# Masks, maxima and output products in fewer VectorE instructions, with finer waits in the norms' moments

## What is computed

```python
def _mha(x, kv, Wq, Wk, Wv, mask, causal):          # block 0, a = 0 and 1
    ...
    lengths = jnp.sum(energy[:, :, 0, :] != 0, axis=-1)
    energy = jnp.where(cols[None, None, None, :] >= lengths[:, :, None, None], -jnp.inf, energy)
...
    scores = jnp.where(key_mask[None, :, None, :] == 0.0, NEG, scores)   # block 3, a = 5 to 7
    attn = jax.nn.softmax(scores, axis=-1)
    query_mask = jnp.sign(jnp.abs(jnp.sum(q, axis=-1)))
    attn = attn * query_mask[None, :, :, None]
    out = jnp.einsum('hbqk,hbkd->hbqd', attn, Vh)
    out = out.transpose(1, 2, 0, 3).reshape(B, Sq, d)
    out = out + q
    return _layer_norm(out, gamma, beta)
```

## Time and profile before

| | |
|---|---|
| median of 3 runs | 1087.1 us (1087.01 to 1087.42) |
| profiled execution, span from first to last instruction | 1085.1 us |
| median above that span | 2.0 us |
| PE busy | 1005.6 us, 93% |
| PEld busy | 725.6 us, 67% |
| DVE busy | 840.9 us, 77%, 2336 instructions |
| ACT busy | 635.8 us, 59% |
| POOL busy | 320.4 us, 30% |

### The profile page before, as it was taken

The page is one execution under the profiler, slowest core; times in us unless marked ns, Lnnn a source line. Parts: engine busy times, 40 slices in busy tenths (PEclk is TensorE's granted clock), DMA queues, the critical chain, the costliest instruction groups (busy, mean ns, idle before and its releaser), DMA issues.

```text
span 1085.1 us, 38818 instructions
## 1 busy us (share of the span) xinstructions
PE 1005.6 (93%) x16923; PEld 725.6 (67%) x16957; DVE 840.9 (77%) x2336; ACT 635.8 (59%) x938; POOL 320.4 (30%) x405
## 2 busy tenths in 40 slices
PE   8889988899999999999999998889999999998996
PEld 5657665576777677767776776556767677677674
DVE  5897999867476756789878899999567774679986
ACT  5346565567777464555645655556777766464652
POOL 4022245511000113346450313553011020336531
PEclk9999999999999999999979999999999999999998
DMA  7000000000000000000010000000000000000001
GB/s 255 3 22 23 2 3 3 2 2 2 3 3 3 12 9 14 11 2 2 2 31 2 3 13 3 2 2 2 3 2 3 3 3 3 1 2 2 2 2 40
DMA packets 13722, 13.60 MB, mean 13 GB/s; under 512 B 617, under 2 KB 13170, under 8 KB 13298
## 3 DMA queue, kind: packets, MB, share of 16 engines
q1 hardware_dynamic: 13554, 11.11, 3.2%
HBM read 9.01 MB, written 2.10 MB: 10 GB/s over the span
## 4 chain that ended last, share of the span: by engine, by line
PE 42%; DVE 28%; ACT 5%; issue 3%; POOL 2%; POOLq 0%; DVEq 0%; ACTq 0%
PE pair L708 8%; DVE mx L1363 7%; PE pair L916 7%; PE pair L911 5%; PE pair L782 4%; PE pair L695 4%; PE pair L935 3%; DVE stats L1085 3%; PE pair L815 2%; DVE Y L1164 2%; ACT PT L1011 2%; PE pair L702 2%; PE pair L683 2%; DVE Y L1108 2%; PE pair L949 2%
## 5 line engine op out<-in xcount | busy, mean ns | idle before, releaser
L1011 ACT ACTIVATE PT<-pair 128x1024 f32<-128x1024 f32 x184 | 180.3, 1029 | 124.8 <-PE pair L916 115.7
L1363 DVE TENSOR_REDUCE mx<-pair 128x16 f32<-128x1024 f32 x184 | 218.4, 1215 | 42.1 <-PE pair L916 41.6
L916 PEld LDWEIGHTS pair<-KQ 32*128 32x128 f32 (+3 forms) x4416 | 170.7, 157 | 37.6 <-DVE mx L1363 3.4
L916 PE MATMUL pair<-KQ 32*128 32x128 f32 (+3 forms) x4416 | 180.0, 254 | 2.4 <-DVE mx L1363 1.0
L708 PE MATMUL pair<-xf,W_all 128*128 128x512 f32 x336 | 177.4, 623 | 3.2 <-ACT xf L977 1.0
L1390 POOL TENSOR_SCALAR ve<-mv 128x4 f32<-128x4 f32 x64 | 17.0, 265 | 503.3 <-DVE mv L1088 432.5
L683 PE MATMUL pair<-warm 128*128 128x512 bf16 (+3 forms) x581 | 113.4, 395 | 17.8 <-DVE Y L1164 7.8
L977 ACT ACTIVATE KQ<-pair,c 128x512 f32<-128x512 f32 x160 | 100.3, 692 | 42.9 <-PE pair L708 42.2
L935 PE MATMUL pair<-PT,V 128*32 128x64 f32 x5120 | 94.2, 221 | 2.2 <-ACT PT L1011 0.7
L977 ACT ACTIVATE V<-pair 64x512 f32<-64x512 f32 x128 | 79.1, 618 | 26.5 <-PE pair L815 24.7
L935 PEld LDWEIGHTS pair<-PT,V 128*32 128x32 f32 x5120 | 78.3, 110 | 22.2 <-issue 8.7
(11 more groups left out here) (122 smaller groups left out, 1824.0 us busy)
## 6 DMA issues: line engine op xcount, KB each, us to landing
W_all<-weights SPq DMA_DIRECT2D x1, 2880.0 KB, 13.7
Xin<-x SPq DMA_DIRECT2D x8, 256.0 KB, 3.6
C<-ctx SPq DMA_DIRECT2D x8, 256.0 KB, 4.1
out<-X SPq DMA_DIRECT2D x8, 256.0 KB, 2.5
row<-rows SPq DMA_DIRECT2D x1, 1024.0 KB, 6.1
c<-const SPq DMA_DIRECT2D x1, 504.0 KB, 5.5
W_all<-weights SPq DMA_DIRECT2D x1, 192.0 KB, 2.9
c<-const SPq DMA_DIRECT2D x1, 80.5 KB, 2.0
```

Source lines behind the costliest of these rows:

```text
L916: last[u] = pe.matmul(banked[u // 2][:, at:at + 2 * S], stationary[rows_, seq].rearrange("p r t -> p (r t)"), moving[rows_, seq].rearrange ...
L1011: act.activation(PT[:, place, :], banks.of("B", a, s, v)[:], ACT.Exp, scale=float((D // (2 * PAIRS[a])) ** -0.5)).then_inc(*banks.drain((" ...
L1363: dve.tensor_reduce(dst, banks.of("A", a, s, v)[:].rearrange("p (u m t) -> p u m t", u=2, t=S), AX.X, ALU.max).then_inc(*banks.drain(("A", ...
```

## The change

The order table is untouched. The edits:

- **moments**: each statistics counts as an event of its own, and each aggregation waits for its own statistics instead of the last. In step z each statistics waits for its own j of X.
- **nm**: one scalar_tensor_tensor over all 128 partitions, mx times -1 times the table half, which is 1 at the partition's own place and 0 at the other; so it also writes the zeros.
- **lm, km**: one tensor_tensor over all 128 partitions each. lm compares with the table place (position at the own place, -1 at the other, where no length is below it) and yields 1; the factor -BIG moves into the tables passed and beyond, which lrow and kms now multiply by. km multiplies by the table gone.
- **outputs** for the last three attentions: rq is left out. Instead of one product of 256 elements there are two of 128 (j apart), each PSUM times qm as a scalar per partition, times rd.
- POOL's 16 memsets of nm8, lm8, nm2, lm2 go, and DVE's wait for them.
- The float constants grow from 161 to 174 columns.

```diff
-CONST32 = [("ident", 128), ("side8", 2), ("side2", 2), ("par8", 2), ("par2", 2), ("pos", 1),
-           ("own", 8), ("half", 2), ("strip", 4), ("rows", 2), ("ownA", 8)]
+CONST32 = [("ident", 128), ("side8", 2), ("side2", 2), ("par8", 2), ("par2", 2), ("place", 2),
+           ("own", 8), ("half", 2), ("strip", 4), ("rows", 2), ("ownA", 8),
+           ("passed", 8), ("beyond", 2), ("gone", 2)]
...
+    c["place"] = np.where(c["half"], (p % S)[:, None], -1)
+    c["passed"], c["beyond"], c["gone"] = -BIG * c["ownA"], -BIG * c["rows"], -ABSENT * c["half"]
...
-                def moments(src, *tag):
+                def moments(src, *tag, made=None):
                     for j in range(NT):
-                        dve.bn_stats(stats[lane(tag)][:, j, :], src[:, j, :]).then_inc(*vec.mark("stats", *tag))
-                    dve.wait_ge(*vec.at("stats", *tag))
+                        if made:
+                            dve.wait_ge(*vec.at(*made, j))
+                        dve.bn_stats(stats[lane(tag)][:, j, :], src[:, j, :]).then_inc(*vec.mark("stats", *tag, j))
                     for j in range(NT):
+                        dve.wait_ge(*vec.at("stats", *tag, j))
                         dve.bn_aggr(mv[lane(tag)][:, j, :], stats[lane(tag)][:, j, :]).then_inc(*vec.mark("mv", *tag))
...
+                    if PAIRS[a] == 2:
+                        o = O[s].rearrange("p j (h d) -> p j h d", h=heads)
+                        for j in range(2):
+                            q = 2 * half + j
+                            dve.scalar_tensor_tensor(out=o[:, q], in0=t[:, j, :, 0:dh], scalar=qm[s][:, q:q + 1],
+                                                     in1=rd[s][:, q, 0:heads].unsqueeze(2).broadcast_to((P, heads, dh)),
+                                                     op0=ALU.mult, op1=ALU.mult
+                                                     ).then_inc(*banks.drain(use, vec, "O", a, s, half))
+                        return
...
-                    if name in ("nm", "lm", "km"):
-                        loaded(pool, "zero", s)
...
-                        dve.wait_ge(*vec.at("x2", a, s))
-                        moments(X[s], "n3", a, s)
+                        moments(X[s], "n3", a, s, made=("x2", a, s))
...
                     elif name == "lm":
-                        for h in range(2):
-                            dve.tensor_scalar(lm8[s][r[h], :, h, :],
-                                              banks.of(*use)[r[h], 0:8 * NB].rearrange("p (n h) -> p n h", h=2),
-                                              K32("pos")[r[h]], -BIG, ALU.is_le, ALU.mult
-                                              ).then_inc(*banks.drain(use, vec, "lm", a, s))
+                        shape = P, 4 * NB, 2, 2
+                        dve.tensor_tensor(lm8[s][:], banks.of(*use)[:, 0:8 * NB].rearrange("p (n h) -> p n h", h=2).unsqueeze(
+                            2).broadcast_to(shape), K32("place").unsqueeze(1).unsqueeze(3).broadcast_to(shape), ALU.is_le
+                            ).then_inc(*banks.drain(use, vec, "lm", a, s))
                     elif name == "km":
-                        for h in range(2):
-                            dve.tensor_scalar(lm2[s][r[h], :, h, :], k[r[h]], -ABSENT, None, ALU.mult
-                                              ).then_inc(*banks.drain(use, vec, "lm", a, s))
+                        shape = P, NB, 2, 2
+                        dve.tensor_tensor(lm2[s][:], banks.of(*use)[:, 0:NB].unsqueeze(2).unsqueeze(3).broadcast_to(shape),
+                                          K32("gone").unsqueeze(1).unsqueeze(3).broadcast_to(shape), ALU.mult
+                                          ).then_inc(*banks.drain(use, vec, "lm", a, s))
                     elif name == "nm":
-                        for h in range(2):
-                            dst = (nm8 if pairs == 8 else nm2)[s][r[h], :, :, h]
-                            src = mx[s][r[h], 0:NB * pairs].rearrange("p (n h) -> p n h", h=2)
-                            dve.tensor_scalar(dst, src, -1.0, None, ALU.mult).then_inc(*vec.mark("nm", a, s))
+                        n = NB * pairs
+                        dve.scalar_tensor_tensor(
+                            out=(nm8 if pairs == 8 else nm2)[s].rearrange("p n r h -> p (n r) h"),
+                            in0=mx[s][:, 0:n].unsqueeze(2).broadcast_to((P, n, 2)), scalar=-1.0,
+                            in1=K32("half").unsqueeze(1).broadcast_to((P, n, 2)), op0=ALU.mult, op1=ALU.mult
+                            ).then_inc(*vec.mark("nm", a, s))
...
-                    for buf in (nm8, lm8, nm2, lm2, V8_padded, V2):
+                    for buf in (V8_padded, V2):
```

More of the change, by code:

```diff
@@ L349, in constants @@
     eye = np.eye(P)
-    c = {"ident": eye, "ones3": (p < 3)[:, None] * np.ones(128), "pos": (p % S)[:, None]}
+    c = {"ident": eye, "ones3": (p < 3)[:, None] * np.ones(128)}
     for n, pairs in (("8", 8), ("2", 2)):
@@ L1161, in outputs @@
                         f = rq
-                    o = O[s][:, two].rearrange("p j (h r d) -> p (j h) r d", r=2, d=dh) if PAIRS[a] == 8 else O[s][
-                        :, two].rearrange("p j (h d) -> p j h d", h=heads)
+                    o = O[s][:, two].rearrange("p j (h r d) -> p (j h) r d", r=2, d=dh)
                     dve.tensor_tensor(o, t[:, :, :, 0:dh], by_head(f).unsqueeze(3).broadcast_to((P, *o.shape[1:])),
@@ L1272, in step @@
                                                      in1=X[s][:, j, :], op0=ALU.mult, op1=ALU.add
-                                                     ).then_inc(*vec.mark("x2", a, s))
-                        dve.wait_ge(*vec.at("x2", a, s))
-                        moments(X[s], "n3", a, s)
+                                                     ).then_inc(*vec.mark("x2", a, s, j))
+                        moments(X[s], "n3", a, s, made=("x2", a, s))
                     elif name == "n3":
@@ L1332, in step @@
                         dve.wait_ge(*banks.ready(*use))
-                        k = banks.of(*use)[:, 0:NB].unsqueeze(2).broadcast_to((P, NB, 2))
-                        for h in range(2):
-                            dve.tensor_scalar(lm2[s][r[h], :, h, :], k[r[h]], -ABSENT, None, ALU.mult
-                                              ).then_inc(*banks.drain(use, vec, "lm", a, s))
+                        shape = P, NB, 2, 2
+                        dve.tensor_tensor(lm2[s][:], banks.of(*use)[:, 0:NB].unsqueeze(2).unsqueeze(3).broadcast_to(shape),
+                                          K32("gone").unsqueeze(1).unsqueeze(3).broadcast_to(shape), ALU.mult
+                                          ).then_inc(*banks.drain(use, vec, "lm", a, s))
                     elif name == "nm":
@@ L1351, in step @@
                                           banks.of(*use)[0:n, 0:S].unsqueeze(1).broadcast_to((n, 8, S)),
-                                          K32("ownA" if name == "lrow" else "own")[0:n, :].unsqueeze(2).broadcast_to(
+                                          K32("own" if name == "mrow" else "ownA" if PAIRS[a] == 2 else "passed")[0:n, :].unsqueeze(2).broadcast_to(
                                               (n, 8, S)), ALU.mult).then_inc(*banks.drain(use, vec, done, a, s))
@@ L1355, in step @@
                             dve.tensor_tensor(kms[s][0:n], banks.of(*use)[0:n, 0:S].unsqueeze(1).broadcast_to((n, 2, S)),
-                                              K32("rows")[0:n, :].unsqueeze(2).broadcast_to((n, 2, S)), ALU.mult
+                                              K32("rows" if PAIRS[a] == 2 else "beyond")[0:n, :].unsqueeze(2).broadcast_to((n, 2, S)), ALU.mult
                                               ).then_inc(*banks.drain(use, vec, "kms", a, s))
```

1 line of the change is left out of this document (removed).

## The result

| | before | after |
|---|---|---|
| median of 4 runs, alternating on one chip | 1087.26 us (1087.01 to 1089.19) | 1057.14 us (1055.88 to 1057.40) |
| ratio | | 0.9727 [0.9706, 0.9748] |
| profiled execution, span | 1085.1 us | 1055.4 us |
| mean granted clock of TensorE in it | 0.986 | 0.994 |
| DVE busy | 840.9 us | 793.3 us |

What follows compares the result with a forecast made beforehand. PE, 93% busy, was taken as the bound, waiting partly on DVE. DVE savings of 56 us x 0.36 gave 20, perhaps 25 us on the path, discounted to 16: 1071 us from 1087.1, range 1062 to 1083.

Steps and rivals of the forecast that it cites:

- What bounds the kernel: Whole span: PE, 93% busy, bounds; DVE savings help mostly in stretches making up 485 of 1085 us.
- Nearly none: Expected sign in 240:640: almost no PE idleness left there, of 63 us over the whole span.
- The size on DVE: All edited DVE parts: 56 us of 841 saved from start to start, DVE busy near 795 us.
- The products' open operand: Last layers' output products, PSUM, SBUF and scalar: 6.1 us saved if no POOL stalls, 4.3 us lost otherwise; gain taken.
- The path: Share of DVE savings on the chain of waits: 0.36 of 56 us, reduced to 16 us off the span.
- The chain sum: DVE savings on the chain of waits: 56 x 0.36 = 20 us, perhaps 25, before any discount.
- The discount for what the next path takes: PE becomes next when DVE comes earlier: middle of two thirds of each bound, 13 and 17, taken as 16 us.
- rival 2: Whole span: the whole chain sum comes through, 25 us and a little more, 1060 us; chance 0.12.
- my own case: Whole span: 16 us faster, 1071 us, within 1063 to 1079; chance 0.62.
- PE did not close up at once: Denies the rival that only stretches with PE below 90% gain: 5 us, 1082 us; chance 0.16.
- Rival 3: Finer waits on DVE: even a met wait bars overlap, so they save nothing, 1074 us; chance 0.06.
- Rival 4: Last layers' output products: both per half stall on POOL over the port, making the kernel slower, 1100 us; chance 0.04.

Runs made afterwards that it cites:

- late pads: Kernel before with the finer waits alone, plus a spare 72-element DVE reduction after the last aggregation in each of 88 moments calls: 1077.52 us, 0.9966.
- n_negmax: Kernel before with only the negated maxima made by one instruction (memsets stay): 1078.33 us, 0.9918.
- am_again: Changed kernel with the moments' coarse waits (for the last statistics) put back, run beside the changed kernel: 1066.51 us, 0.9817.
- an_halves: Changed kernel with the negated maxima in two partition halves again, with their memsets: 1067.14 us, 0.9864.

## Why the prediction was wrong

**What bounds the kernel: right.** The gain lies where DVE is dense, and PE closed most of it up elsewhere. "Nearly none" of PE's idleness in 240:640 was too strong: 10 of the 57.7 us are there, and the largest part (24 us) is in 0:240, which I had not named.

**The size on DVE: right.** The sum of 56 us from start to start meant a busy time near 795; it is 793.3. By parts the single kernels show busy time down by 12.0 (finer waits; 11.5 forecast, of which 3 are gaps), 18.9 (nm; 24.6, of which some 4 are gaps), 11.6 (masks; 13.9, some 2.4 gaps) and 3.9 (products; 6.1, some 1.7 gaps). The 12.0 hold the 3 us that are not the edit's. nm takes 284 and 192 ns in the median for 0.28 and 0.18, the small lm 186 for 0.18, the products 347 for 0.344, lm 287 for 0.28.

**The products' open operand: the bound taken was right.** 96 instructions lie between 341 and 352 ns, though 37 of them run beside a POOL operation of over 0.6 us. So neither PSUM with one SBUF tensor nor the scalar per partition beside them waits for POOL.

**The path: the first step that failed.** The chain sum was "56 x 0.36 = 20 us, and perhaps 25", and then "the middle of two thirds of each bound ... 16 us". At equal clock the change gives 22.9 us (1080.5 - 1057.6; 23.3 and 23.7 within a group), between the two undiscounted numbers, a share of 22.9/56 = 0.41. The discount for what the next path takes was the mis-sized term: it made 16 of what measured 23. My reading is that the share of the chain holds already what the next path takes, since the chain runs through PE wherever PE is later, and that I took it off a second time; no run tests this by itself. The late pads, which add no gaps, give 0.38 to 0.49 for the share: more than the discounted 16/56 = 0.29, but not fine enough to tell 0.36 from 0.41. What I put down as rival 2, with 0.12, came nearer than my own case. The parts' shares of busy time scatter widely, from 0.26 (masks) to 0.95 (products), so one share serves at best a sum over many places, not one edit.

**The clock, a term put at nothing: the step that took the time out of the range.** With the discount left out and nothing else, the forecast would have been 1087.1 - 22.9 = 1064, within 1062 to 1083. The other 7 us of the 30 go with the granted clock, on which the prediction has no word. The profile I summed against had a clock of 0.986 and a 14 us stretch at half clock, and the runs shown with it (1087.0 to 1087.4) lie where executions at 0.988 lie on average; other executions of the same kernel at 0.994, which is the clock of the profile after, take 1080.1 us. The row of clocks in the profile showed the 7, and I did not ask what it cost. The time follows the clock over executions; no run sets the clock and looks at the time. Whether the change itself raises the clock is not settled: the changed kernel had medians of 0.994 to 0.997 in its three groups, the kernel before 0.988 to 0.992 in four, and 0.992 and 0.990 beside the changed one's 0.994 and 0.996; but n_negmax had 0.983 and am_again 0.990. So the 7 us may be luck of the executions compared, or in part the change's own.

**The rivals.** PE did not close up at once. Rival 3 fell: a met wait bars no overlap, the aggregations have 0.0 us idle, and the finer waits, worth nothing by this rival, gave 8.4 us alone, and cost 3.4 and 4.9 where the changed kernel went without them. The Trainium skill's sentence named there (VectorE: DVE Perf Modes, The DRAIN you can't avoid), that the next operation waits for the empty pipe and semaphores cost nothing extra, does not hold here; the section's other sentence, that a next operation which is not held starts earlier, does: what costs is a wait for the instruction just ahead, 0.12 to 0.14 us each time. Rival 4, the slower one, has no trace at all.

## What to carry to other kernels

Before taking something off a share of the chain of waits for the next path, ask whether the chain has not passed through that path already: here the share as read (0.36) came nearer to the measured 0.41 than the discounted 0.29, in one kernel. Before summing against a profiled execution, read its row of clocks and compare several executions: here 0.008 of mean clock was a quarter of the result. When a warm-up or filling instruction is added, look in the trace whether it runs in the gap or behind it. When two small DVE instructions step from one half of the partitions to the other, or read two SBUF tensors beside a busy POOL, look at their maximum and not their mean: one instruction over all partitions, or one input left in PSUM, takes the long ones away.

## What the runs showed of the hardware

- The mean granted clock of TensorE differs between executions of the same kernel, 0.986 to 0.998 in 49 executions, and the time with it, 0.7 to 1 us per 0.001 at 1080 us.
- PE was idle for 1.3 to 1.5 us at the same place in all 18 profiles, and a stretch of 10 us or more at half clock began there in three.
- A DVE step to other partitions, with nothing to wait for, leaves a gap of 0.03 us and loses the overlap of 0.08; the second half stands up to 1.27 us behind a POOL operation that starts 0.03 to 0.10 us before it (seven of 64 second halves, in the kernel before as in an_halves). Of two instructions over all partitions no second one did so, in 64.
- A DVE instruction with one PSUM tensor, one SBUF tensor and a scalar per partition never stalled on POOL (96 and 32 instructions, all of 341 to 352 ns, 37 and 22 of them beside a POOL operation); with both tensors in SBUF it went up to 1434 ns.
